# A mixture of experts on one core in split fp32: x forms spread out, additions over two pairs, old down products moved up, tail reordered

## The reference, cut to what matters

```python
E, B, S, D, F = (8, 2, 256, 256, 1024)      # here x is (16, 256, 256): 16 batches
g = jnp.einsum('bsd,edf->ebsf', h, Wg)
u = jnp.einsum('bsd,edf->ebsf', h, Wu)
expert_outs = jnp.einsum('ebsf,efd->ebsd', jax.nn.silu(g) * u, Wd)
expert_output = jnp.einsum('be,ebsd->bsd', gating_probs, expert_outs)
shared = jnp.einsum('bsf,fd->bsd', jax.nn.silu(h @ Sg) * (h @ Su), Sd)
out = x + (1.0 - sg) * expert_output + sg * shared      # all in fp32
```

## Time and profile before

| | |
|---|---|
| device time, median of 3 runs | 2184.05 us (2183.82 to 2184.12) |
| the profiled execution's own time | 2182.51 us |
| its span | 2180.7 us |
| TensorE busy | 2144.4 us (98%), 9180 matmuls |
| VectorE, ScalarE, GpSimd busy | 1468.7, 1305.7, 1612.9 us |
| TensorE in the chain that ended last | 96% |
| 16 DMA engines, share of the span | 52.9% |

### The profile page before, as it was taken

The page is one execution under the profiler, slowest core; times in us unless marked ns, Lnnn a source line. Parts: engine busy times, 40 slices in busy tenths (PEclk is TensorE's granted clock), DMA queues, the critical chain, the costliest instruction groups (busy, mean ns, idle before and its releaser), DMA issues.

```text
span 2180.7 us, 34110 instructions
## 1 busy us (share of the span) xinstructions
PE 2144.4 (98%) x9180; PEld 1722.5 (79%) x9180; DVE 1468.7 (67%) x2643; ACT 1305.7 (60%) x2336; POOL 1612.9 (74%) x1432
## 2 busy tenths in 40 slices
PE   7999999999999999999999999999999999999998
PEld 5888888888777888888877788888887888888886
DVE  6666666666677666666677666666667666666666
ACT  6777777677565555555556555555555555555554
POOL 7987787777288777777778777777777777777775
PEclk9999999999999999999999999999999999999999
DMA  8676666666454554454454554455445455445542
GB/s 302 227 248 219 244 222 233 228 226 223 182 202 173 201 201 171 184 202 190 170 195 172 202 202 182 173 200 202 170 183 197 167 212 202 184 172 199 202 174 115
DMA packets 122449, 433.73 MB, mean 199 GB/s; under 512 B 13728, under 2 KB 41504, under 8 KB 122400
## 3 DMA queue, kind: packets, MB, share of 16 engines
q1 hardware_dynamic: 122400, 433.19, 52.9%
HBM read 329.85 MB, written 103.28 MB: 199 GB/s over the span
## 4 chain that ended last, share of the span: by engine, by line
PE 96%; DVE 2%; issue 1%; DMA 0%; POOL 0%; ACT 0%; SPq 0%; ACTq 0%; DVEq 0%; POOLq 0%
PE chain_ps L542 15%; PE chain_ps L544 14%; PE chain_ps L543 14%; PE down_ps L542 8%; PE down_ps L544 7%; PE down_ps L543 7%; PE p_ps L542 6%; PE p_ps L543 6%; PE p_ps L544 6%; PE side_ps L542 4%; PE side_ps L544 4%; PE side_ps L543 4%; DVE h_forms L965 1%; DVE acc L962 0%; DMA w_raw<-w 0%
## 5 line engine op out<-in xcount | busy, mean ns | idle before, releaser
L384 POOL TENSOR_TENSOR h_forms<-h_t,h_forms 128x512 fp32r<-128x512 f32 x431 | 564.7, 1330 | 281.7 <-ACT h_forms L848 281.7
L542 PE MATMUL chain_ps<-x_hi,gate_forms 128*128 128x512 f32 x1080 | 429.3, 398 | 15.0 <-DVE silu L962 13.3
L544 PE MATMUL chain_ps<-x_hi,gate_forms 128*128 128x512 f32 x1080 | 426.2, 395 | 0.0
L543 PE MATMUL chain_ps<-x_lo,gate_forms 128*128 128x512 f32 x1080 | 424.0, 393 | 0.0
L384 POOL TENSOR_TENSOR h_t<-h_b,h_t 128x512 f32<-128x512 f32 x214 | 314.6, 1470 | 95.6 <-DVE h_b L956 90.6
L962 DVE TENSOR_TENSOR p_ps<-tap_p,chain_ps 128x512 f32<-128x512 f32 x216 | 150.4, 696 | 266.2 <-PE chain_ps L544 266.2
L865 ACT COPY chain_ps<-chain_ps 128x512 f32<-128x512 f32 x216 | 123.1, 570 | 291.0 <-DVE h_a L956 201.3
L848 ACT CAST h_forms<-h_t 128x512 fp32r<-128x512 f32 x432 | 268.4, 622 | 17.9 <-POOL h_t L384 5.2
L384 POOL TENSOR_TENSOR w_lo<-w_raw,w_hi 128x1152 fp32r<-128x1152 f32 x71 | 191.0, 2691 | 96.9 <-ACT w_hi L765 94.9
L542 PEld LDWEIGHTS chain_ps<-x_hi,gate_forms 128*128 128x128 f32 x1080 | 202.7, 188 | 68.0 <-DVE silu L962 17.0
L544 PEld LDWEIGHTS chain_ps<-x_hi,gate_forms 128*128 128x128 f32 x1080 | 202.6, 188 | 50.5
(11 more groups left out here) (105 smaller groups left out, 4918.4 us busy)
## 6 DMA issues: line engine op xcount, KB each, us to landing
gate_forms<-kept_gate SPq DMA_DIRECT2D x216, 896.0 KB, 7.3
down_forms<-kept_down SPq DMA_DIRECT2D x108, 896.0 KB, 4.6
kept_gate<-w_hi SPq DMA_DIRECT2D x72, 448.0 KB, 2.5
kept_gate<-w_lo SPq DMA_DIRECT2D x72, 448.0 KB, 3.0
w_raw<-w SPq DMA_DIRECT2D x72, 256.0 KB, 3.2
w_raw<-w SPq DMA_DIRECT2D x72, 128.0 KB, 2.9
kept_down<-d_hi SPq DMA_DIRECT2D x36, 256.0 KB, 2.9
kept_down<-d_lo SPq DMA_DIRECT2D x36, 256.0 KB, 2.9
```

Of the source, the lines that this page charges most:

```text
L384: return nc.gpsimd.tensor_tensor(dst, a, b, ALU.subtract)
L542: nc.tensor.matmul(bank, w_high, hi, start=start, stop=False, **on)
L543: nc.tensor.matmul(bank, w_high, lo, start=False, stop=False, **on)
L544: return nc.tensor.matmul(bank, w_low, hi, start=False, stop=stop, **on)
```

## The change

Five edits:

1. `probs_sb`, `shared_sb`, `routed_part`, `coef` and `warm` are allocated after the large tensors. `w_raw` and all behind it start 1248 bytes lower in each partition: at a multiple of 64 bytes, where it was 32 over one.
2. The three tables of the x forms have only even chunk numbers, up to 22. For this the first three experts of a group are written out on GpSimd and ScalarE, not two.
3. In the first pair of group 1, the old down products of tile 0 chunk 6 and tile 1 chunk 7 all stand before `p6`; those of tile 0 chunk 7 at the places of q6 and q4; three places are empty. `add(0)` moves to the second pair.
4. In groups 2 and 3, `finish_q(4)`, the two additions from `u3_sum`, `finish_q(2)` and `finish_q(3)` move from the first pair to three places of the second.
5. In the tail `h_t2` and `h_t3` are made ahead of `h0`, GpSimd takes over the lo form of `T4` and the two additions from `u3_sum`, and `finish_q(5)` waits for these.

```diff
 B11, T1, B21, T2, B22, T3, T4 = range(7)
-X_SUM_AT = {4: T1, 5: T2, 6: T3, 7: T4}
-X_HI_AT = {5: B11, 6: T1, 7: B21, 8: T2, 9: B22, 10: T3, 11: T4}
-X_LO_AT = {8: B11, 9: T1, 10: B21, 11: T2, 12: B22, 13: T3, 14: T4}
+X_SUM_AT = {2: T1, 4: T2, 6: T3, 8: T4}
+X_HI_AT = {6: B11, 8: T1, 10: B21, 12: T2, 14: B22, 16: T3, 18: T4}
+X_LO_AT = {10: B11, 12: T1, 14: B21, 16: T2, 18: B22, 20: T3, 22: T4}
+X_EXPERTS = 3
...
-        probs_sb = sb("probs_sb", [P, BATCH, ROUTED])
...
         h_forms = sb("h_forms", [P, 2 * X_FORMS, TOKENS], F32R)
+
+        probs_sb = sb("probs_sb", [P, BATCH, ROUTED])
...
             form_lo_of(T2, 6, LAST_PAIR + 1)
             form_lo_of(T3, 7, LAST_PAIR + 1)
+            form_lo_of(T4, 4, LAST_PAIR + 1)
+            pool.wait_ge(tapped[7], LAST_PAIR)
+            for t in range(2):
+                a = acc[:, 2 * (GROUPS - 1) + t, 1, :]
+                nc.gpsimd.tensor_tensor(a, u3_sum[:], a, ALU.add).then_inc(u3_added, 1)
...
                 p1(na, ka)
                 p5(na, ka)
                 down_step(1, 0, CHUNKS - 2, 0)
+                if opening:
+                    for tile, k, c in ((0, CHUNKS - 2, 1), (1, CHUNKS - 1, 0), (1, CHUNKS - 1, 1)):
+                        down_step(None, tile, k, c)
                 p6(na, ka)
-                down_step(5, 0, CHUNKS - 2, 1)
+                down_step(5, None, None, None)
                 p2(ka)
                 p7(na, ka)
                 p3(ka)
                 p1(nb, kb)
                 p4(g, ka, na, first=first)
-                down_step(6, 1, CHUNKS - 1, 0)
+                down_step(6, 0, CHUNKS - 1, 0)
                 p5(nb, kb)
-                down_step(4, 1, CHUNKS - 1, 1)
+                down_step(4, 0, CHUNKS - 1, 1)
                 p6(nb, kb)
                 p2(kb)
-                down_step(7, 0, CHUNKS - 1, 0)
+                down_step(7, None, None, None)
                 p7(nb, kb)
                 p3(kb)
-                down_step(2, 0, CHUNKS - 1, 1)
+                down_step(2, None, None, None)
                 down_step(3, None, None, None)
 
             for k in range(CHUNKS):
...
 
                 dve.wait_ge(q_done[number], pc + 1)
                 if number == 7 and first:
+                    after(dve, u3_added, 2 * (g - 1))
                     ins = nc.vector.tensor_copy(u3_sum[:], side_ps[:])
                 else:
                     into = {1: acc[:, 2 * g, 0, :], 6: acc[:, 2 * g + 1, 0, :], 7: u3_sum[:]}[number]
...
                 u4(na, ka)
                 if not opening:
                     tap(1, gp, pc - 1, False)
+                if second and g == 1:
+                    add(0)
+                elif second:
+                    finish_q(4, g - 1, [acc[:, 2 * (g - 1), 1, :]])
                 up1(na, ka)
                 if opening:
                     dve.wait_ge(w_lo_done, PER - 1)
...
                     tap(6, gp, pc - 1, False)
                 if first and g > 1:
                     finish_q(5, gp, [acc[:, 2 * gp + 1, c, :] for c in range(DC)])
+                if second and g > 1:
+                    dve.wait_ge(tapped[7], (g - 1) * PER_PAIRS)
+                    dve.wait_ge(finished[4], g - 1)
+                    for t in range(2):
+                        a = acc[:, 2 * (g - 1) + t, 1, :]
+                        plus(a, u3_sum[:], a).then_inc(u3_added, 1)
                 u4(nb, kb)
                 if not opening:
                     form_lo_of(B21, pc)
                     tap(7, gp, pc - 1, is_first(ep, jp))
                 else:
                     add(1)
-                if first and g == 1:
-                    pass
-                elif first:
-                    finish_q(4, gp, [acc[:, 2 * gp, 1, :]])
-                    dve.wait_ge(tapped[7], gp * PER_PAIRS)
-                    dve.wait_ge(finished[5], gp)
-                    for t in (1, 0):
-                        if t == 0:
-                            dve.wait_ge(finished[4], gp)
-                        a = acc[:, 2 * gp + t, 1, :]
-                        plus(a, u3_sum[:], a).then_inc(u3_added, 1)
-                    finish_q(2, gp, [acc[:, 2 * gp, 0, :]])
-                    finish_q(3, gp, [acc[:, 2 * gp + 1, 0, :]])
-                if opening:
-                    add(0)
+                if second and g > 1:
+                    finish_q(2, g - 1, [acc[:, 2 * (g - 1), 0, :]])
+                    finish_q(3, g - 1, [acc[:, 2 * (g - 1) + 1, 0, :]])
 
             def coefficients():
...
                 form_lo_of(B11, count)
                 up1(LAST, kb)
                 h1(g, e, LAST, p53_ps[:])
-                h0(g, e, kb, LAST, up0)
                 dve.wait_ge(h_summed[T1], count)
                 dve.wait_ge(h1_done, LAST + 1)
                 minus(h_t2[:], p53_ps[:], h_t1[:]).then_inc(h_summed[T2], 1)
                 minus(h_t3[:], p53_ps[:], h_a1[:]).then_inc(h_summed[T3], 1)
+                h0(g, e, kb, LAST, up0)
                 dve.wait_ge(h_summed[T2], count)
                 dve.wait_ge(h0_done, LAST + 1)
                 minus(h_t4[:], up0, h_t2[:]).then_inc(h_summed[T4], 1)
+                form_lo_of(B22, count, full=p53_ps[:])
                 tap(1, g, LAST_PAIR, False)
-                form_lo_of(B22, count, full=p53_ps[:])
                 form_lo_of(B21, count, full=up0)
-                form_lo_of(T4, count)
                 tap(6, g, LAST_PAIR, False)
+                dve.wait_ge(u3_added, 2 * g)
                 finish_q(5, g, a[1])
-                dve.wait_ge(tapped[7], LAST_PAIR)
-                dve.wait_ge(finished[5], g)
-                for t in range(2):
-                    plus(a[t][1], u3_sum[:], a[t][1]).then_inc(u3_added, 1)
                 finish_q(3, g, [a[1][0]])
                 dve.wait_ge(q_done[7], count)
-                dve.wait_ge(u3_added, 2 * g)
+                dve.wait_ge(finished[5], g)
                 for t in (1, 0):
                     plus(a[t][1], side_ps[:], a[t][1]).then_inc(tapped[7], 1)
                 finish_q(2, g, [a[0][0]])
```

More of the change, by code:

```diff
@@ L71, in moe_kernel @@
         u3_sum = sb("u3_sum", [P, TOKENS])
-        probs_sb = sb("probs_sb", [P, BATCH, ROUTED])
-        shared_sb = sb("shared_sb", [P, BATCH])
-        routed_part = sb("routed_part", [P, BATCH])
-        coef = sb("coef", [P, EXPERTS * BATCH])
-        warm = sb("warm", [P, 1])
         with ExitStack() as opening_only:
@@ L121, in moe_kernel @@
         h_forms = sb("h_forms", [P, 2 * X_FORMS, TOKENS], F32R)
+        probs_sb = sb("probs_sb", [P, BATCH, ROUTED])
+        shared_sb = sb("shared_sb", [P, BATCH])
+        routed_part = sb("routed_part", [P, BATCH])
+        coef = sb("coef", [P, EXPERTS * BATCH])
+        warm = sb("warm", [P, 1])
         h_sum = {T1: h_t1, T2: h_t2, T3: h_t3, T4: h_t4}
@@ L473, in prepare @@
                     down_lo(e, k // 2)
-                if isinstance(e, int) and e < 2:
+                if isinstance(e, int) and e < X_EXPERTS:
                     next_x(0, e, k)
@@ L485, in h_pair @@
                 n, pc = group(g, e, 2 * j), pair(g, e, j)
-                static = isinstance(e, int) and e < 2
+                static = isinstance(e, int) and e < X_EXPERTS
                 started = not isinstance(pc, int) or pc > 0
@@ L516, in h_pair @@
                 form_lo_of(T1, 5, pc + 1)
-            for e in range(2):
+            for e in range(X_EXPERTS):
                 for k in range(CHUNKS):
                     prepare(e, k)
-            with pool.Fori(2, EXPERTS - 1) as e:
+            with pool.Fori(X_EXPERTS, EXPERTS - 1) as e:
                 for k in range(CHUNKS):
@@ L526, in _ @@
             for g in range(1, GROUPS):
-                for e in range(2):
+                for e in range(X_EXPERTS):
                     for j in range(PAIRS):
                         h_pair(g, e, j)
-                with pool.Fori(2, EXPERTS) as e:
+                with pool.Fori(X_EXPERTS, EXPERTS) as e:
                     for j in range(PAIRS):
@@ L920, in _ @@
             down_hi(0, 0)
-            for e in range(2):
+            for e in range(X_EXPERTS):
                 for k in range(CHUNKS):
                     unit(e, k)
-            with act.Fori(2, EXPERTS - 1) as e:
+            with act.Fori(X_EXPERTS, EXPERTS - 1) as e:
                 for k in range(CHUNKS):
@@ L929, in _ @@
             for g in range(1, GROUPS):
-                for e in range(2):
+                for e in range(X_EXPERTS):
                     for j in range(PAIRS):
                         two_groups(g, e, j)
-                with act.Fori(2, EXPERTS) as e:
+                with act.Fori(X_EXPERTS, EXPERTS) as e:
                     for j in range(PAIRS):
```

## The result

| | before | after |
|---|---|---|
| device time, median | 2183.94 us (2180.85 to 2184.12, 4 runs) | 2124.15 us (2123.18 to 2125.27, 4 runs) |
| ratio, 95% interval | | 0.973 (0.9713 to 0.9746) |
| span of the profiled run | 2180.7 us | 2122.1 us |

The account below looks back on a forecast made before the run. TensorE was taken as the bound, busy 2144.4 of 2180.7 us, so ordering could win at most 36.3 us. Terms of -4.5, -2.9, -1.3, -3.4 and -0.2 sum to -12.3: 2184.05 to 2171.7 us, range 2168 to 2177.5.

Parts of the forecast that it names:

- Small tensors last: Tensors from `w_raw` on move down 1248 bytes, no instruction changes: 0 us, outside 0 +- 1 us.
- if the matmul's 0.2321 changes: Sign that the prediction is wrong: TensorE's matmuls no longer take 0.2321 us each.
- Old down products ahead of the seed: First pair of group 1: three more products fill the 1.72 us seed wait; 1.3 of 4.23 us stay, -2.9 us.
- the clock behind it: Matmuls at half clock between 585 and 600 us go once the waits before them shrink: -1.3 us, bounds 0 and -1.3.
- Final additions over two pairs: Groups 2 and 3: five additions move to the second pair; 2.9 of 6.30 us of waits stay, -3.4 us.
- Rival A: Given back at the borders: moved additions cost the second pair what they cost the first; 2177.6 us, chance 0.14.
- X forms over twelve pairs: GpSimd steps leave the second half of pairs, so four TensorE waits go: -4.5 us, bounds 0 to -4.5.
- rival C: The x forms' waits stay, since they hang on hundredths, and the rest comes: 2176.2 us, chance 0.12.
- rival B: Slower: first-half steps push `h_t<-h_a` into `h_forms<-h_b`, holding both forms in 22 pairs; 2201 us, chance 0.04.
- The tail: `h_t2` and `h_t3` first, GpSimd takes two additions: -0.2 us, between +0.8 and -1.
- The sum of the order: All terms together, -4.5 - 2.9 - 1.3 - 3.4 - 0.2 = -12.3 us, with 0 for the placement.
- rival E: More than forecast: the second pairs are nearly free, 2167 us, chance 0.07.

Follow-up runs that it names:

- move_only: The kernel before with only the five small tensors allocated last, nothing reordered: 2138.83 us, ratio 0.9783.
- before_pad800: The kernel before, old order and small tensors in their old place, with one unused tensor of 800 bytes ahead of `w_raw`: 2137.0 us, ratio 0.9782.
- old_borders: The kernel after with the five final additions back in the first pair, in their old order: 2131.35 us, ratio 0.9763.
- old_opening: The kernel after with the old down products at their old places and both old additions in the first pair of group 1: 2128.21 us.
- order_only: The kernel after with the small tensors left in their old place, all other edits in: 2168.66 us, ratio 0.9926 against the kernel before.
- x_off64: The kernel after with `x_hi` and `x_lo` alone starting 64 bytes off the other operands of TensorE: 2157.7 us.

## Why the prediction was wrong

**The step that failed** is "Small tensors last": "I take 0 ... Outside: 0 +- 1 us". It measured 45 to 48 us, by `move_only` and `before_pad800`. The step named what no row shows, a weight load at another start, and then took its bound from GpSimd's 1.28 and 1.29 us. GpSimd isn't the engine that bounds the kernel, and its row says nothing of how TensorE reads. A bound for TensorE was to be had from the rows shown. At the lower clock matmuls start 0.43 us apart, in `old_borders` (1091.04 - 1088.05)/7 = 0.427: that is 512 columns at 1.2 GHz with nothing on top. At 2.4 GHz 512 columns are 0.2133, and the 0.2319 of the earlier trace rows has 0.0186 us more. Nothing in the profile says what these are. Over 9180 matmuls they are 171 us. An edit that moves the operands of every one of them may take away any part of that, and no row bounds what it may add. The Trainium skill states a much smaller remainder (TensorE: Matmul & The Clock Gate, Back-to-back issue gap): start to start for a matmul taken by itself is the columns by the clock exactly at 1.2 GHz, and some 2.5 ns more at 2.4 GHz, which makes 215.8 ns for 512 columns. The first half agrees with the 0.427; the second doesn't, neither before nor after, and the 16 ns between it and the 0.2319 were a sign that could have been read. For a stream with a weight load to each matmul the same section gives some 131 ns at 512 columns; no stretch here comes near that, the shortest mean distance is 226.5. The 0 stood for "no instruction changes", which isn't the same as "no instruction takes another time". The prediction did name the sign by which it would be wrong, "if the matmul's 0.2321 changes", but gave it no chance.

**Old down products ahead of the seed, and the clock behind it**: right. -2.9 and -1.3 were forecast, and `old_opening` measures 4.1. The seed is there in time. The forecast left 1.3 us of waiting in three pieces: two new waits of 0.25 for `u4`, and so 0.8 for `silu`. After, the two for `u4` are 0.50 - 0.23 = 0.27 each and the one for `silu` is 0.78, 1.3 in all. With the old order the waits of 1.83 and 2.52 come back, and a half clock too, but behind the first of them, where the kernel before had it behind the second; `before_pad800`, with the old order as well, has none there. So the 1.3 us of the clock hold for some executions and not for others.

**Final additions over two pairs**: right in mechanism, too small in size. Forecast -3.4. In the old placement the waits left are those of `order_only` for `u4` and for an addition,

```profile
PE chain_ps L549 <- DVE p_ps L972: 0.7, 1, 0.7
PE down_ps L549 <- DVE acc L972: 0.5, 2, 0.2
```

and a late `p4` behind either second pair, which starts 0.46 behind its predecessor, 0.23 more than it need. That is 1.7 us against 2.9 forecast to stay of 6.30. The place was right (the two from `u3_sum` take 2.86 us against GpSimd, and `u4` is late), its size was little more than half. In the new placement the edit is worth 7.2, since `old_borders` has the half clock at both borders besides. Rival A, given back at the borders, is out.

**X forms over twelve pairs**: right in mechanism, but not a term of its own. Forecast -4.5, and indeed none of the four waits is left in `order_only`, so rival C is out. After, no `h_forms<-h_b` in pairs 1 to 11 of group 1 takes over 1.1 us, so rival B didn't come. But with the old tables put back, only 2.6 us are lost in the old placement and nothing in the new one. With the new borders the two waits of group 2 don't come with the old tables either, and the new tables bring the wait in the second pair of group 2, which the prediction had booked under the borders. The four waits were taken as independent of the rest, and they aren't.

**The tail**: forecast -0.2, measured -0.3, inside what the runs can tell.

**The sum of the order** was 12.3. `order_only` measures 16 (12.7 to 19.9), its span 15.1; in the new placement it is 12.9 to 14.7. The start of the same matmul in the traces of before and `order_only` shows where the 15.1 lie: 4.6 in the opening pairs (forecast 4.2), 5.7 where the x waits were (4.5), 4.0 at the two borders (3.4), 0.1 in the tail (0.2), and 0.7 in the first 30 us, where the order is the same. So the three larger terms came out somewhat above their forecasts; a wait costs a little more than the idle time in its brackets. Taken alone the order would have given 2168 us, at the lower end of the range and near rival E's number. So the miss is in the main one term, and that term was priced from the wrong engine's row.

## What to carry to other kernels

Where TensorE bounds, compare the distance of its starts with its columns at the granted clock; what is over is a term of its own, and what an edit that moves operands can win is bounded by it. Before ordering work by hand, see whether the tensors which TensorE reads start alike modulo 256 bytes (tried here for 128 x 128 x 512 matmuls in rounded fp32 alone): one unused tensor of 800 bytes gave here some three times what the whole reordering gave. An experiment on order should hold the placement still, or the two can't be told apart.

## What was not expected of the hardware

- The start distance of 128 x 128 x 512 matmuls in rounded fp32 is 0.2265 to 0.2274 us in kernels whose operands all start alike modulo 256 bytes, and from 0.2310 to 0.2330 in the others between 700 and 1050 us. At the lower clock it is 0.43 in either. That it is TensorE's own two reads that meet (the 512 columns and the next weights) is a guess that would fit these distances, but it doesn't say why like matmuls behind unlike ones are slow, and it wasn't shown. Group 3 of `x_off64` excludes other engines' use of x as the cause, but not their use of other tensors.
- The weight load's own duration doesn't show it. Its rows before and after, with the same mean of 188 ns:

```profile
L542 PEld LDWEIGHTS chain_ps<-x_hi,gate_forms 128*128 128x128 f32 x1080 | 202.7, 188 | 68.0 <-DVE silu L962 17.0
```

```profile
L549 PEld LDWEIGHTS chain_ps<-x_hi,gate_forms 128*128 128x128 f32 x1080 | 202.5, 188 | 60.9 <-ACT chain_ps L875 8.1
```

- The granted clock fell behind a wait of 3.23 us in `old_borders` and not behind one of 3.15 us before, with the same order on either side; in `old_opening` it fell behind one of 1.83 us, where before it held. The plainest case is one execution of `before_pad800`, with a wait of 3.23 us at each of two borders and the same order: behind the first the granted clock is 1.00, behind the second 0.61.

```profile
1092.40:1096.80 4.40, 4.19 (x18) 3.49 (x19) 3.32 (x7) 2.37 (x5) 3.04 (x3) 1.00 0.98 345
1613.00:1617.40 4.40, 4.19 (x11) 3.33 (x12) 2.50 (x6) 1.43 (x3) 3.04 (x3) 0.61 0.93 342
```

So the length of a wait doesn't tell it. A saved wait of 3.2 us can be worth half as much again.
